# A mixture-of-experts stage with its loops written out, and one tile fewer

## The chip, the cores and the metric

The kernel runs on one core of a Trainium2 chip. The metric is the device time of one execution in microseconds (us). A core has five engines with programs of their own: TensorE (PE, matrix products; PEld is its weight load), VectorE (DVE), ScalarE (ACT), GpSimd (POOL) and SyncE (SP), which here does nothing but issue transfers. They wait for each other on semaphores.

## What is computed

One transformer layer on x of 4 x 1024 tokens of width 128, all in float32:

```python
x = _layernorm(x + attn(x, W_Q, W_K, W_V, W_O))     # 16 heads, rope, causal
gate_probs = softmax(x @ Wg + bg)                   # 8 experts
_, top_idx = top_k(gate_probs, 2)
selected = gate_probs * one_hot(top_idx).sum(-2)
selected = selected / (selected.sum(-1, keepdims=True) + 1e-08)
h = gelu(einsum('bsf,efh->bseh', x, W1) + b1)       # hidden width 512
expert_out = einsum('bseh,ehf->bsef', h, W2) + b2
x = _layernorm(x + einsum('bsef,bse->bsf', expert_out, selected))
```

## The kernel before

**Before the expert stage.** Attention runs as a long list of events, with batches 1 and 2 as two turns of a hardware loop. During it the router finds two experts for each token, and POOL scatters a row for each of the 8192 (token, expert) pairs into the DRAM buffer `pairs`, sorted by expert. This fills most of the time up to 568 us of the profiled execution.

**Tiles.** The expert stage works on tiles of 128 pairs that belong to one expert. 8192 pairs make 64 full tiles, and each of 8 experts can leave one more that is not full, so at most 64 + 8 - 1 = 71 tiles hold pairs. `NTILE` is this number rounded up to a whole turn of `TL` = 8 tiles: 72. Tiles count from 0; turn t is tiles 8t to 8t+7. Which expert a tile belongs to and where its rows stand is worked out on DVE (`word`, `expert`). The first `EARLY` = 40 tiles are filled from batches 0 to 2, and run while the routing of batch 3 is still going on; tiles from 40 on need all pairs.

**A tile's way.** SP (`load_pairs`, L606 to L614) reads the tile's word from memory into a register, waits until buffer k = tile mod 8 is free (`ys_ready` of the tile 8 before), then issues two transfers: the expert's weights W1 with biases into `w1e` (L612, 322 KB) and the 128 rows into `xg` (L613, 66 KB; the trace calls xg `region`). PE then does three things with each tile, and in one step of its program they belong to three tiles: `stage_down` of tile i (L832: reads the expert's number; L837: four products), `stage_up` of tile i+2 (L848: four products) and `stage_tx` of tile i+3 (L857: a transpose of the rows; it waits for the load). ACT copies the transpose (L923) and does four gelus, one for each quarter (L931). DVE (`stage_y`, L1357 to L1363) adds b2 and multiplies by the gate; POOL (`stage_out`, L1528) scatters the rows to `results`.

**The turns.** `pipeline` writes this out for each engine. A turn in which other work stands at fixed tiles (`TILE_EVENTS`: routing of batch 3 in turns 0 to 3, the sums of batches 0 to 2 at tiles 64 to 71), turn 4 and the last turn are written out tile by tile, so every number in them is a constant. Turns 5, 6 and 7 (tiles 40 to 63) are a hardware loop `Fori` of 8 tiles; there each semaphore count is `turn * 8 + k`, with the turn in a register. On SP the loads of tiles 8 to 31 and of tiles 40 to 63 are two such loops. Between them stand turn 4's loads, each followed by a transfer that pads one expert's rows (L633, L634), and a wait for all scatters (L636 to L638).

**The end.** After its load of tile 65, SP waits for the results of tiles up to 55 (L646) and reads the results of batch 0 back (`load_back`, L618, two transfers of 512 KB), after tiles 67 and 69 those of batches 1 and 2. POOL adds the first half of each (`FIRST`, L1511), DVE the second (`SECOND`, L1341), and DVE takes the statistics (`SUM`, L1346). `SCALES` makes the layernorm factors of batches 0 to 2, with which ACT normalises them (L943). When all results are out (L651), batch 3 is read back and treated in the same way (DVE L1372 to L1383).

Of the kernel before, what the change touches and what calls it, by code (L numbers as in the profile page):

```python
# [26 lines left out]
P = 128  # L27
B, S, D = 4, 1024, 128
H, DK = 16, 8
E, HID = 8, 512  # L30
# [15 lines left out]
GATE_EPS = 1e-8  # L46
TL = 8

NTILE = -(-(2 * B * S // P + E - 1) // TL) * TL
CAPT = B * S // P + 1  # L50
SPARE = NTILE - 2 * B * S // P

EARLY = (2 * (B - 1) * BT - (E - 1)) // TL * TL
LATE = NTILE - EARLY

OLD = -(-(2 * (B - 1) * BT + E - 1) // TL) * TL
# [159 lines left out]
def tile_events():  # L216

    groups = []
    for e, r in EVENTS[END + 1:]:
        if e[0] == "TILE":  # L220
            groups.append([])
        else:
            groups[-1].append((e, r))
    chain = [g for g in groups if g[0][0][0] != "SC"]
    plan = {}
    for i, g in enumerate(chain):
        plan.setdefault(2 * i // 3, []).extend(g)
    first = 2 * (len(chain) - 1) // 3 + 1
    scatters = [e for g in groups if g[0][0][0] == "SC" for e in g]
    for i, e in enumerate(scatters):  # L230
        plan.setdefault(first + i // 2, []).append(e)
    for i in range(4):
        plan.setdefault(first + i, []).append((("TB", i), None))
    done = max(plan)
    assert done < EARLY - TL + 2

    tail = {8: [("FIRST", 0)], 9: [("SECOND", 0), ("FIRST", 1)], 10: [("SUM", 0, 0), ("SUM", 0, 1)],
            11: [("SECOND", 1), ("FIRST", 2)], 12: [("SUM", 1, 0), ("SUM", 1, 1)], 13: [("SECOND", 2)],
            14: [("SUM", 2, 0), ("SUM", 2, 1)], 15: [("SCALES",), ("FIRST", B - 1)]}
# [40 lines left out]
def build(nc, xT, x, w, wg, bg, w1, w2,  # L280
          cs, ident, halves, maskA, before, tile128, tokens, tiles, first_row, out):
    ctx = ExitStack()
    with ctx:
# [199 lines left out]
        def _(sp):  # L483
# [121 lines left out]
            def load_pairs(turn, k):  # L605
                both = sp.value_load(word[0:1, bass.ds(turn * TL + k, 1)], min_val=0, max_val=E * PLACES - 1)  # L606
                t = (both & (PLACES - 1)).with_bounds(min_val=0, max_val=E * CAPT + SPARE - 1)
                e = (both >> 9).with_bounds(min_val=0, max_val=E - 1)
                if not (isinstance(turn, int) and turn == 0):
# [11 lines left out]

            sp.wait_ge(tiles_ready, 1)
            sp.wait_ge(pv_done, NB * (NU - 1))
            for k in range(TL):
                load_pairs(0, k)
            with sp.Fori(1, EARLY // TL - 1) as turn:
                for k in range(TL):
                    load_pairs(turn, k)

            sp.wait_ge(pad_ready, 1)  # L630
            for e_ in range(E):
# [4 lines left out]
            sp.wait_ge(tiles_ready, 2)  # L636
            sp.wait_ge(spare_in, 16 * (1 + E))
            sp.wait_ge(pairs_out, 16 * 2 * NT)  # L638
            with sp.Fori(EARLY // TL, NTILE // TL - 1) as turn:
                for k in range(TL):  # L640
                    load_pairs(turn, k)
            for k in range(TL):
# [21 lines left out]
        def _(pe):  # L664
# [187 lines left out]
            def stage_tx(turn, k):  # L852

                pe.wait_ge(pair_in[k], turn * 32 + 32)
                if not (isinstance(turn, int) and turn == k == 0):
# [154 lines left out]
        def _(ve):  # L1010
# [344 lines left out]
            def stage_y(turn, k):  # L1355
                ve.wait_ge(y_done, turn * TL + (k + 1))
                v.tensor_tensor(yb[:, k % 2, :], down[k % 2],  # L1357
                                w1e[:, k, HID + HC:HID + HC + D], ALU.add).then_inc(y_read, 1)
                if not (isinstance(turn, int) and turn == 0):
# [174 lines left out]

def first_use(turn, k):

    return isinstance(turn, int) and turn == 0 and k < 2


def first_late(turn, k):  # L1540

    return isinstance(turn, int) and turn * TL + k == EARLY


def pipeline(eng, stages, visit):

    lead = max(n for _, n in stages)
    turns = NTILE // TL

    for t in range(-lead, 0):  # L1550
        for stage, n in stages:
            if 0 <= t + n:
                stage(0, t + n)
    def whole(turn):
        for k in range(TL):
# [8 lines left out]
    single = {i // TL for i in TILE_EVENTS} | {EARLY // TL - 1, turns - 1}  # L1564
    turn = 0
    while turn < turns:
        if turn in single:
            whole(turn)
            turn += 1
        else:  # L1570
# [53 lines left out]
```

## Time and profile before

| | us |
|---|---|
| median of 3 runs | 769.34 |
| lowest, highest | 766.18, 774.05 |
| profiled execution, span | 795.5 |
| PE busy in the profiled execution | 670.2 (84%) |
| DVE busy | 570.4 (72%) |
| ACT busy | 443.8 (56%) |
| POOL busy | 351.2 (44%) |

All times in the text that are not called a run are those of the profiled execution, from the start of its span. The columns of each view are told where its first rows stand.

### The profile page before, as it was taken

Reading aid. Unit: us, or ns where it says so; the run is one execution under the profiler, and the core shown is the slowest. Engines: PE = TensorE matmul, PEld = TensorE weight load, DVE = VectorE, ACT = ScalarE, POOL = GpSimd, SP = SyncE. Lnnn points to the kernel's source line nnn. Section 1 sums busy time; section 2 is a strip of 40 time slices with the busy share of each in tenths; the row PEclk is TensorE's granted clock in tenths of the full one; section 3 lists DMA queues with packets and bytes.
Section 4 is the critical chain, followed back from the end, with each engine's and each line's share of the span. In section 5 each row is a group of like instructions: output and inputs, shape, how many; then the busy total and the mean of one; then the engine's idle time right before and its main releaser. Section 6 shows DMA issues by size and latency. Waiting matters only on the chain.

```text
span 795.5 us, 19063 instructions
## 1 busy us (share of the span) xinstructions
PE 670.2 (84%) x5560; PEld 362.2 (46%) x5561; DVE 570.4 (72%) x1386; ACT 443.8 (56%) x843; POOL 351.2 (44%) x664
## 2 busy tenths in 40 slices
PE   7879999999898897989898998898698766999950
PEld 3344333334343332434333334332198756888840
DVE  8977888888879886787988898986255621222295
ACT  2343676666555665555567656567456433655535
POOL 5862224223353484153447516248423555444460
PEclk9985999999989999898999999999799977999995
DMA  8883455011010120101012001000276745687935
GB/s 288 271 287 130 141 136 157 18 49 49 2 49 2 56 79 22 49 1 49 6 55 83 28 33 48 1 8 29 66 217 185 198 123 151 186 212 204 298 89 158
DMA packets 67358, 83.75 MB, mean 105 GB/s; under 512 B 9266, under 2 KB 46776, under 8 KB 67264
## 3 DMA queue, kind: packets, MB, share of 16 engines
q1 hardware_dynamic: 62912, 74.04, 31.5%
q0 software_dynamic: 4352, 8.53, 3.1%
q8 instruction: 49, 0.80, 0.5%
q14 instruction: 45, 0.37, 0.2%
HBM read 55.77 MB, written 26.90 MB: 104 GB/s over the span
## 4 chain that ended last, share of the span: by engine, by line
PE 53%; DVE 21%; issue 10%; ACT 4%; SPq 3%; DMA 3%; POOL 2%; another core or an unknown queue 1%; DVEq 0%; ACTq 0%; POOLq 0%
PE banks L779 15%; DVE mx L1226 12%; PE banks L729 9%; PE banks L759 6%; PE banks L837 5%; PE banks L848 5%; PE banks L724 3%; ACT region L895 2%; PE banks L671 2%; PE banks L788 2%; DMA region<-pairs 1%; DVE region L1363 1%; PE banks L686 1%; ACT region L931 1%
## 5 line engine op out<-in xcount | busy, mean ns | idle before, releaser
L1226 DVE TENSOR_REDUCE mx<-banks 128x1 f32<-128x512 f32 (+3 forms) x640 | 365.2, 631 | 52.3 <-PE banks L729 47.6
L895 ACT ACTIVATE region<-banks 128x1024 f32<-128x1024 f32 (+3 forms) x256 | 201.5, 841 | 136.8 <-PE banks L759 132.1
L729 PE MATMUL banks<-region 64*128 64x512 bf16 (+3 forms) x768 | 188.4, 340 | 13.8 <-DVE mx L1226 10.8
L759 PE MATMUL banks<-region 64*128 64x512 bf16 (+3 forms) x768 | 139.2, 339 | 12.0 <-ACT region L895 5.5
L779 PE MATMUL banks<-region 128*32 128x512 f32 (+3 forms) x1024 | 118.8, 537 | 0.9 <-POOL region L1518 0.8
L1528 POOL DMA_INDIRECT results<-region,dest x72 | 71.5, 993 | 105.8 <-DVE region L1363 83.8
L895 ACT ACTIVATE cs_sb<-banks 128x1024 f32<-128x1024 f32 (+2 forms) x128 | 91.2, 759 | 43.2 <-PE banks L759 42.4
L724 PE MATMUL banks<-mask_sb,half_sb 64*128 64x128 bf16 (+1 forms) x384 | 83.3, 249 | 25.4 <-DVE mx L1226 19.8
L1518 POOL TENSOR_SCALAR_AFFINE_SELECT region<-region 128x256 f32<-128x256 f32 x160 | 63.8, 407 | 84.0 <-ACT region L895 80.6
L848 PE MATMUL banks<-region,w1e 128*128 128x128 f32 x576 | 84.0, 293 | 20.0 <-ACT region L923 15.2
L1357 DVE TENSOR_TENSOR region<-banks,w1e 128x128 f32<-128x128 f32 x72 | 20.9, 290 | 105.6 <-PE banks L837 60.0
L1518 POOL TENSOR_SCALAR_AFFINE_SELECT cs_sb<-cs_sb 128x256 f32<-128x256 f32 x96 | 38.0, 408 | 128.6 <-ACT cs_sb L895 127.8
L759 PEld LDWEIGHTS banks<-region 64*128 64x128 bf16 x768 | 42.1, 94 | 112.8 <-issue 41.9
L837 PE MATMUL banks<-w_sb,region 128*128 x576 | 83.7, 291 | 7.9 <-DVE region L1357 3.1
L848 PEld LDWEIGHTS banks<-region,w1e 128*128 128x128 f32 x576 | 76.4, 207 | 22.3 <-ACT region L923 17.0
L729 PEld LDWEIGHTS banks<-region 64*128 64x128 bf16 x768 | 63.3, 98 | 49.4 <-DVE mx L1226 34.7
L931 ACT ACTIVATE region<-banks,w1e 128x128 f32<-128x128 f32 x288 | 82.6, 378 | 0.5 <-PE banks L848 0.5
L837 PEld LDWEIGHTS banks<-w_sb,region 128*128 128x128 f32 x576 | 74.4, 201 | 12.9 <-issue 11.5
L1503 POOL DMA_INDIRECT pairs<-xT_sb,slot x64 | 63.0, 985 | 24.4 <-issue 15.0
L923 ACT COPY region<-banks 128x128 f32<-128x128 f32 x72 | 19.2, 266 | 94.5 <-PE banks L857 62.2
L726 PE MATMUL banks<-mask_sb,half_sb 64*128 64x64 bf16 (+1 forms) x384 | 70.1, 207 | 0.0
L724 PEld LDWEIGHTS banks<-mask_sb,half_sb 64*128 64x128 bf16 x384 | 34.8, 97 | 62.4 <-DVE mx L1226 44.8
(204 smaller groups left out, 705.9 us busy)
## 6 DMA issues: line engine op xcount, KB each, us to landing
w1e<-in_w SPq DMA_DIRECT2D x72, 322.0 KB
region<-stack_q SPq DMA_DIRECT2D x64, 112.0 KB
region<-stack_k SPq DMA_DIRECT2D x32, 224.0 KB
region<-pairs SPq DMA_DIRECT2D x72, 66.0 KB
region<-results SPq DMA_DIRECT2D x8, 512.0 KB, 4.8
stack_q<-x_sb SPq DMA_DIRECT2D x8, 384.0 KB, 3.7
stack_k<-x_sb SPq DMA_DIRECT2D x8, 384.0 KB, 4.6
stack_q<-x_sb SPq DMA_DIRECT2D x8, 256.0 KB, 3.6
```

Source lines behind the costliest of these rows:

```text
L724: mm(view[:, :, n - P:n], half_sb[rows, 0, :], mask_sb[rows, 0, 0:k, :], start=True, stop=False, skip_group_check=True)
L726: mm(view[:, :, n - P // 2:n], half_sb[rows, 1, :], mask_sb[rows, 1, 0:k, P // 2:P], start=False, stop=False, skip_group_check=True)
L729: last = mm(ring[:, bank, m * n:(m + 1) * n], qst[rows, v % NG, sb_ // 4, slot_, sb_ % 4 * P:(sb_ % 4 + 1) * P], kst[rows, v % NG, slot_, ...
L759: last = mm(score[:, slot_, par, 0:n], kst[rows, u % NG, slot_, j * P:(j + 1) * P], qst[rows, u % NG, c, slot_, s0 - c * CH:s0 - c * CH + ...
L779: last = mm(pv[32 * h:32 * h + 32, s0 - c * CH:s0 - c * CH + n], vx[:, u % NG, j, h, :], probs[(2 * e[1] + slot_) % 6][:, par, 0:n], start ...
L837: last = mm(down[k % 2], hg[:, k % 2, hc * P:(hc + 1) * P], w2_sb[:, bass.ds(e, 1), hc, :].rearrange("p a n -> p (a n)"), start=(hc == 0), ...
L848: last = mm(hidden[k % 2][:, hc * P:(hc + 1) * P], w1e[:, k, hc * P:(hc + 1) * P], xgT[:, k % 2, :], start=(hc == 0), stop=(hc == HC - 1), ...
L895: nc.scalar.activation(probs[i % 6][:, :, 0:n], score[:, i % 2, :, 0:n], ACT.Exp, scale=SCALE).then_inc(exp_done, 1)
L931: nc.scalar.activation(hg[:, k % 2, cols], hidden[k % 2][:, cols], ACT.Gelu_apprx_tanh, bias=w1e[:, k, HID + hc:HID + hc + 1]).then_inc(ge ...
L1226: read(v.tensor_reduce(dst, src, AX.X, ALU.max, negate=True))
L1518: pp.affine_select(out=block_, in_=block_, compare_op=ALU.is_ge, fill=0.0, base=0, pattern=[[0, 2], [1, P]], channel_multiplier=-1).then_i ...
L1528: pp.indirect_dma_start(out=results, out_offset=bass.IndirectOffsetOnAxis(ap=dest[:, k, :], axis=0), in_=ys[:, k, :], in_offset=None, boun ...
```

## The change

`NTILE` becomes 71. All engines' turns are written out: `pipeline` has no loop any more, and so have SP's loads. `SCALES` and `FIRST` of batch 3 move from tile 71 to tile 70, behind that tile's `SUM`.

```diff
-NTILE = -(-(2 * B * S // P + E - 1) // TL) * TL
+NTILE = 2 * B * S // P + E - 1
...
-            14: [("SUM", 2, 0), ("SUM", 2, 1)], 15: [("SCALES",), ("FIRST", B - 1)]}
+            14: [("SUM", 2, 0), ("SUM", 2, 1), ("SCALES",), ("FIRST", B - 1)]}
...
-            with sp.Fori(EARLY // TL, NTILE // TL - 1) as turn:
-                for k in range(TL):
-                    load_pairs(turn, k)
-            for k in range(TL):
-                load_pairs(NTILE // TL - 1, k)
-                if k == 1:
+            for t in range(EARLY, NTILE):
+                load_pairs(t // TL, t % TL)
+                if t == NTILE // TL * TL + 1:
                     for i in range(TL):
                         sp.wait_ge(result_out[i], 16 * (OLD // TL))
-                if k in (1, 3, 5):
-                    load_back(k // 2)
+                if t - NTILE // TL * TL in (1, 3, 5):
+                    load_back(t % TL // 2)
 
             for k in range(TL):
-                sp.wait_ge(result_out[k], 16 * (NTILE // TL))
+                sp.wait_ge(result_out[k], 16 * (NTILE // TL + (k < NTILE % TL)))
...
-    for t in range(-lead, 0):
+    for t in range(-lead, NTILE):
         for stage, n in stages:
-            if 0 <= t + n:
-                stage(0, t + n)
-    def whole(turn):
-        for k in range(TL):
-            for stage, n in stages:
-                if not isinstance(turn, int) or turn * TL + k + n < NTILE:
-                    stage(turn + (k + n) // TL, (k + n) % TL)
-            if isinstance(turn, int):
-                for e, r in TILE_EVENTS.get(turn * TL + k, []):
-                    visit(e, r, lambda n, stride: n)
...
-            end = min(i for i in single if i > turn)
-            with eng.Fori(turn, end) as i:
-                whole(i)
-            turn = end
+            if 0 <= t + n < NTILE:
+                stage((t + n) // TL, (t + n) % TL)
+        for e, r in TILE_EVENTS.get(t, []):
+            visit(e, r, lambda n, stride: n)
```

On PE, the first tile of the loop's body before, from the loop's entry: the read of the expert's number, `stage_down`, and the beginning of `stage_up`. `REGISTER_ALU` and `ISA` are register instructions.

```order
2904 L1572 ISA
2905 L832 TENSOR_LOAD expert
2906 L832 ISA x2
2907 L834 REGISTER_ALU
2908 L836 ISA [waits y_read]
2909 L837 ISA [waits gelu_done]
2910 L837 MATMUL banks<-w_sb,region 128x128
2911 L836 REGISTER_ALU
2912 L837 ISA [waits gelu_done]
2913 L837 MATMUL banks<-w_sb,region 128x128
2914 L836 REGISTER_ALU
2915 L837 ISA [waits gelu_done]
```

The same piece of PE's program in the change, for a tile of the turns that were in the loop (its lines are 5 lower):

```order
2707 L827 TENSOR_LOAD expert
2708 L827 ISA x2
2709 L832 ISA [waits gelu_done,y_read]
2710 L832 MATMUL banks<-w_sb,region 128x128
2711 L832 ISA [waits gelu_done]
2712 L832 MATMUL banks<-w_sb,region 128x128
2713 L832 ISA [waits gelu_done]
2714 L832 MATMUL banks<-w_sb,region 128x128
2715 L832 ISA [waits gelu_done]
```

Gone are one register instruction ahead of each quarter's product, and others ahead of the first; the products, their number and their order are the same.

On SP, the last load of the loop's body before, the loop's end, and the first load of the last turn, which was written out already:

```order
504 L606 ISA
505 L606 TENSOR_LOAD word
506 L606 ISA x2
507 L612 ISA [waits ys_ready]
508 L612 DMA w1e<-in_w 128x644
509 L613 REGISTER_ALU
510 L613 ISA
511 L613 DMA region<-pairs 128x132
512 L639 REGISTER_ALU
513 L639 COMPARE_AND_BRANCH
514 L606 TENSOR_LOAD word
```

In the change every load has the form that the last turn's loads had:

```order
732 L607 TENSOR_LOAD word
733 L607 ISA x2
734 L613 ISA [waits ys_ready]
735 L613 DMA w1e<-in_w 128x644
736 L614 REGISTER_ALU
737 L614 ISA
738 L614 DMA region<-pairs 128x132
```

A load in the loop had a register instruction ahead of the read, most had another ahead of the wait, and every eighth had the branch.

## Rows read from the trace of the kernel before

**Rows 1.** The page: its span, its engines (busy us, share, instructions), one of its queues.

```profile
span 795.5 us, 19063 instructions
...
PE 670.2 (84%) x5560; PEld 362.2 (46%) x5561; DVE 570.4 (72%) x1386; ACT 443.8 (56%) x843; POOL 351.2 (44%) x664
...
q8 instruction: 49, 0.80, 0.5%
```

**Rows 2.** Chain of waits, 625 to 660 us: start, length, what the end waited for.

```profile
630.86 10.73 another core or an unknown queue
```

**Rows 3.** Timeline of PE: start, us, line, operation [idle before]; L857 is one per tile.

```profile
676.32 0.27 PE L857 MATMUL banks<-id_sb,region 128*128 128x128 f32 x1
...
687.69 0.27 PE L857 MATMUL banks<-id_sb,region 128*128 128x128 f32 x1
...
690.21 0.33 PE L857 MATMUL banks<-id_sb,region 128*128 128x128 f32 x1 [0.46 <-DMA region<-pairs]
...
693.02 0.27 PE L857 MATMUL banks<-id_sb,region 128*128 128x128 f32 x1
...
700.54 0.27 PE L857 MATMUL banks<-id_sb,region 128*128 128x128 f32 x1
...
712.84 0.27 PE L857 MATMUL banks<-id_sb,region 128*128 128x128 f32 x1
...
718.29 0.27 PE L857 MATMUL banks<-id_sb,region 128*128 128x128 f32 x1
...
741.99 0.27 PE L857 MATMUL banks<-id_sb,region 128*128 128x128 f32 x1
...
749.10 0.33 PE L857 MATMUL banks<-id_sb,region 128*128 128x128 f32 x1 [0.89 <-DMA region<-pairs]
...
752.81 0.42 PE L857 MATMUL banks<-id_sb,region 128*128 128x128 f32 x1
```

**Rows 4.** Stretch: busy us (instructions) of PE, PEld, DVE, ACT, POOL; clock, DMA share, GB/s.

```profile
674.30:687.69 13.39, 13.39 (x122) 13.39 (x121) 4.34 (x22) 9.15 (x35) 6.87 (x7) 1.00 0.59 168
```

**Rows 5.** Timeline of SP: weight loads of tiles 2, 3, then 42, 43, then 65.

```profile
575.65 0.33 SPq L612 DMA_DIRECT2D w1e<-in_w  x1
...
577.37 0.33 SPq L612 DMA_DIRECT2D w1e<-in_w  x1
...
690.84 0.33 SPq L612 DMA_DIRECT2D w1e<-in_w  x1
...
692.72 0.33 SPq L612 DMA_DIRECT2D w1e<-in_w  x1
...
740.04 0.17 SPq L612 DMA_DIRECT2D w1e<-in_w  x1
```

**Rows 6.** Waits of SP, 560 to 790: for what, us in total, times, longest.

```profile
SPq L612 <- DVE region L1363: 9.1, 6, 3.6
```

**Rows 7.** Timeline of DVE at the end.

```profile
754.91 0.29 DVE L1357 TENSOR_TENSOR region<-banks,w1e 128x128 f32<-128x128 f32 x1 [2.91 <-PE banks L837]
...
770.52 0.29 DVE L1357 TENSOR_TENSOR region<-banks,w1e 128x128 f32<-128x128 f32 x1
...
782.07 2.36 DVE L1372 TENSOR_TENSOR x_sb<-x_sb,region 128x512 f32<-128x512 f32 x2 [4.92 <-DMA region<-results]
```

**Rows 8.** Timeline of POOL at the end.

```profile
772.18 0.97 POOL L1528 DMA_INDIRECT results<-region,dest  x1 [0.84 <-DVE region L1363]
774.01 0.97 POOL L1528 DMA_INDIRECT results<-region,dest  x1 [0.86 <-DVE region L1363]
```

**Rows 9.** Timeline of PE at the first end of the attention loop's turn.

```profile
312.93 0.39 PE L759 MATMUL banks<-region 64*128 64x512 bf16 x2 [2.81 <-issue]
```

**Rows 10.** DMA queues, 309 to 314: packets, MB, share of 16 engines.

```profile
q8 instruction: 2, 0.03, 2.9%
```

**Rows 11.** DMA queues, 713 to 746, all that moved anything.

```profile
q1 hardware_dynamic: 5779, 6.46, 72.0%
q0 software_dynamic: 451, 0.81, 6.6%
```

More of the change, by code:

```diff
@@ L238, in tile_events @@
             11: [("SECOND", 1), ("FIRST", 2)], 12: [("SUM", 1, 0), ("SUM", 1, 1)], 13: [("SECOND", 2)],
-            14: [("SUM", 2, 0), ("SUM", 2, 1)], 15: [("SCALES",), ("FIRST", B - 1)]}
+            14: [("SUM", 2, 0), ("SUM", 2, 1), ("SCALES",), ("FIRST", B - 1)]}
+    assert max(tail) == NTILE - 1 - OLD
     for i, events in tail.items():
@@ L608, in load_pairs @@
                 e = (both >> 9).with_bounds(min_val=0, max_val=E - 1)
-                if not (isinstance(turn, int) and turn == 0):
+                if turn > 0:
                     sp.wait_ge(ys_ready, turn * TL + (k + 1 - TL))
@@ L623, in _ @@
             sp.wait_ge(pv_done, NB * (NU - 1))
-            for k in range(TL):
-                load_pairs(0, k)
-            with sp.Fori(1, EARLY // TL - 1) as turn:
-                for k in range(TL):
-                    load_pairs(turn, k)
+            for t in range(EARLY - TL):
+                load_pairs(t // TL, t % TL)
             sp.wait_ge(pad_ready, 1)
@@ L638, in _ @@
             sp.wait_ge(pairs_out, 16 * 2 * NT)
-            with sp.Fori(EARLY // TL, NTILE // TL - 1) as turn:
-                for k in range(TL):
-                    load_pairs(turn, k)
-            for k in range(TL):
-                load_pairs(NTILE // TL - 1, k)
-                if k == 1:
+            for t in range(EARLY, NTILE):
+                load_pairs(t // TL, t % TL)
+                if t == NTILE // TL * TL + 1:
                     for i in range(TL):
                         sp.wait_ge(result_out[i], 16 * (OLD // TL))
-                if k in (1, 3, 5):
-                    load_back(k // 2)
+                if t - NTILE // TL * TL in (1, 3, 5):
+                    load_back(t % TL // 2)
             for k in range(TL):
-                sp.wait_ge(result_out[k], 16 * (NTILE // TL))
+                sp.wait_ge(result_out[k], 16 * (NTILE // TL + (k < NTILE % TL)))
             load_back(B - 1)
@@ L854, in stage_tx @@
                 pe.wait_ge(pair_in[k], turn * 32 + 32)
-                if not (isinstance(turn, int) and turn == k == 0):
+                if turn or k:
                     pe.wait_ge(xgT_ready, turn * TL + k)
@@ L1358, in stage_y @@
                                 w1e[:, k, HID + HC:HID + HC + D], ALU.add).then_inc(y_read, 1)
-                if not (isinstance(turn, int) and turn == 0):
+                if turn > 0:
                     ve.wait_ge(result_out[k], turn * 16)
@@ L1535, in first_use @@
 def first_use(turn, k):
-    return isinstance(turn, int) and turn == 0 and k < 2
+    return turn == 0 and k < 2
 def first_late(turn, k):
-    return isinstance(turn, int) and turn * TL + k == EARLY
+    return turn * TL + k == EARLY
 def pipeline(eng, stages, visit):
     lead = max(n for _, n in stages)
-    turns = NTILE // TL
-    for t in range(-lead, 0):
+    for t in range(-lead, NTILE):
         for stage, n in stages:
-            if 0 <= t + n:
-                stage(0, t + n)
-    def whole(turn):
-        for k in range(TL):
-            for stage, n in stages:
-                if not isinstance(turn, int) or turn * TL + k + n < NTILE:
-                    stage(turn + (k + n) // TL, (k + n) % TL)
-            if isinstance(turn, int):
-                for e, r in TILE_EVENTS.get(turn * TL + k, []):
-                    visit(e, r, lambda n, stride: n)
[L1564 to L1570, printed above, removed]
-            end = min(i for i in single if i > turn)
-            with eng.Fori(turn, end) as i:
-                whole(i)
-            turn = end
+            if 0 <= t + n < NTILE:
+                stage((t + n) // TL, (t + n) % TL)
+        for e, r in TILE_EVENTS.get(t, []):
+            visit(e, r, lambda n, stride: n)
 def kernel(L0_attn_x, L0_attn_W_Q, L0_attn_W_K, L0_attn_W_V, L0_attn_W_O, L0_ffn_Wg, L0_ffn_bg,
```

## The prediction, made before the change was run

> **What bounds the kernel now.** I read the page first. PE is the busiest engine, with 84% of a span of 795.5 us [rows 1], and most of that is attention, which the change does not touch. Then I read the chain of waits over the expert stage. Its largest piece is 10.73 us at 630.86 in which nothing that the profile shows was waited for [rows 2]. The median of the runs is 769.34, 26 us under the profiled span, so 26 us of the profiled execution are not in the timed ones. I take stalls of this kind for most of them and claim nothing from them. This one lies in turns that were written out already.
>
> The question is then what one tile costs in each turn. PE's transpose L857 comes once a tile, so its starts in PE's timeline are a clock of the stage. In turn 4, written out before, it goes from 676.32 to 687.69 in 6 tiles: 1.895 us a tile [rows 3]. Over that stretch PE is busy 13.39 of 13.39 us at the full clock [rows 4]. So a written-out turn runs at PE's own work, and no other engine holds it.
>
> From tile 40 on this changes. Tile 40's transpose waits 0.46 us for its load, at 690.21 (SP had pads and a wait for all scatters ahead of it). From tile 41 at 693.02 to tile 63 at 741.99 it takes 48.97 us for 22 tiles, 2.23 a tile. A calm piece inside a turn, 700.54 to 712.84, is 6 tiles in 12.30 us: 2.05 a tile. The two tiles behind it, where the first turn ends, take 5.45 us (to 718.29) [rows 3].
>
> **The change, part by part.**
>
> *Register work of the loop on PE.* 2.05 against 1.895 is 0.155 us a tile. The order listing has a register instruction ahead of the `stage_down` products and more at the other waits, and nothing else differs for PE between turn 4 and these turns: same products, same waits. 22 tiles by 0.155 = 3.4 us. In the change this costs nothing, as in turn 4.
>
> *The turns' ends.* 48.97 - 22 x 2.05 = 3.9 us remain. 1.35 of it stand around the first turn's end (5.45 - 2 x 2.05). From 693.02 to 700.54 3 tiles take 7.52 us, 1.37 over the loop's pace: that is PE getting its lead back after tile 40, with loads that arrive one by one. The rest, 1.15, is spread over the second and third turn. I claim the first turn's end (1.35), half of the rest (0.6), and a quarter of the restart (0.35), as SP's faster loads help there: 2.3 us. Together 5.7 us, of at most 48.97 - 41.69 = 7.3.
>
> *Loads.* Where SP waits for nothing, one written-out load takes 1.72 us (575.65 to 577.37), and one in the loop 1.88 (690.84 to 692.72) [rows 5]. For tiles 8 to 31 the 0.16 us buy nothing: SP waits there for free buffers, 9.1 us in six waits [rows 6], and what it gains it waits longer. Without that cover it would be 24 x 0.16 = 3.8 us. From tile 40 on SP has little lead. At 1.88 it is faster than PE's 2.05, at 1.72 faster than 1.895, by about the same, so PE's pace is not SP's. It matters at one place. Tile 65's load is issued at 740.04, tile 66's comes behind the two read-back transfers, and PE stands 0.89 us for it at 749.10. From 741.99 to 749.10 3 tiles take 7.11 us, 1.4 more than at 1.895, and the next takes 3.71 (752.81), 1.8 more [rows 3]. Bounds: 0, if in timed runs SP is in time anyway, and 3.2, if all this lateness goes. SP took 49.2 us from tile 42 to tile 65, 2.14 a tile where undisturbed loads take 1.88; if that is disturbance that only the profiled run has, SP is in time in the others. The term is then nearer its lower end, and I take 1.0.
>
> *One tile fewer.* In the last turn DVE goes from tile 65's `stage_y` at 754.91 to tile 70's at 770.52, 3.1 us a tile [rows 7]; its `SECOND` and `SUM`, and waits beside POOL's `FIRST`, lie between. So DVE sets the end there, not PE. Tile 71 comes last with no sum beside it: POOL's scatters of tiles 70 and 71 start at 772.18 and 774.01 [rows 8], and the wait for all results hangs on the last. This removes 1.83 us. Bounds: 0.6, DVE's and POOL's part alone if they ran side by side (two operations of 0.29), and 3.1, a mean tile of that stretch; the pair of scatters is the nearest row.
>
> *`SCALES` one tile earlier.* DVE stands 4.92 us before the read-back of batch 3 arrives at 782.07 [rows 7]. Both `SCALES`, ahead of this wait, and the read-back move by the same tile. Cost nothing; if `SCALES` came 4.92 us later it would begin to show. `FIRST` of batch 3 on POOL waits for that read-back anyway.
>
> *More code.* The three turns are three times as long in memory. The trace shows what a fetch costs when it is in the way: at the first turn end of the attention loop PE stands 2.81 us with "issue" as the reason [rows 9], and two packets of the instruction queue q8 fall into this stretch [rows 10]. In the expert loop, from 713 to 746, only q1 and q0 move anything [rows 11]: no code was fetched at its turns. Turn 4 is straight code at PE's full pace, so I cost the straight code at nothing, with a bound of 2.81 for each block that comes late.
>
> The Trainium skill (Runtime: NRT & Kernel Launch, "Instruction fetch mechanics") says that engines prefetch code in sequence, and that a taken branch to code outside the window at hand forces a fetch first. For the attention loop the trace agrees (2.81 us). Held against the expert loop, two taken branches would cost 5.6 us instead of the 1.95 that I claim at turn ends, and the time would be 757.1; the rows of the queues speak against it here.
>
> **Sum:** 3.4 + 2.3 + 1.0 + 1.8 = 8.5 us. Against the profile's own span, 795.5 - 8.5 = 787.0. The terms are tiles at an undisturbed pace, so I carry them over whole to the runs: 769.34 - 8.5 = 760.8 us, 1.1% faster. All of it must get through to the end. It does if the last turn moves as a whole: the read-backs are issued behind tile 65's load, which comes earlier with both PE and SP, and DVE's stretch starts when tile 64 and the first read-back are there.
>
> **Rivals.**
>
> *The loop's cost was hidden, and only the tile counts.* For it: SP delivered at 2.14 us a tile, near PE's 2.23, and q1 fills 72% of the DMA engines' time [rows 11], so PE may have followed the loads. Against it: PE's timeline has one wait for a load in these turns, the 0.46 at tile 40. Then 1.8 us and perhaps a third of the rest (6.7 / 3 = 2.2) are gained: 765.3, within 1%.
>
> *The slower one: code comes late.* Place: turns 5 to 8, on PE or SP, when transfers of loads and read-backs stand before the code's. Price: 2.81 us a block. PE's two extra turns are 16 tiles of 17 products and 17 weight loads, 544 instructions; q8 moved 49 packets for PE's 11,121 [rows 1], so two or three more, and SP's may be as many. With three late nothing is left of the gain; with six, 769.34 - 8.5 + 16.9 = 777.7, slower by 1.1%. Against it: turn 4 and most of attention are straight code that came in time.
>
> *More is gained.* Tile 66's load is late in the timed runs as well, and all loss at turns goes: 7.3 + 3.2 + 1.8 = 12.3, 757.0.
>
> **How the numbers follow.** Main case, 758.5 to 764: 0.55. Hidden cost, 764 to 768: 0.22. More, under 758.5: 0.15. Late code: 0.08, mostly above 768. The predicted time is 760.8. The range for 8 in 10 goes from 756.5, the larger gain with 0.5 for the spread of the runs, to 767.5, the tile alone; it leaves out most of the late code and the edges of its neighbours, 0.18. A measurement of this kernel can tell about 1% from no change, and 1% is at 761.65. Of the main case 0.34 lies below it, with the larger gain 0.49: faster. Slower, above 777: 0.04. The same: 0.47.
>
> **What would show it.** L857 should go at 1.90 us from tile 41 to 63, in under 43.5 us, with no gap at tiles 48 and 56, and SP's loads at 1.72 where nothing is waited for: that proves the first 5.7 us. A pace of 2.05 with PE waiting for `xg` would prove the first rival; gaps with "issue" beside instruction packets, the second. Tile 66's transpose without a wait, where before it had one, proves the 1.0. The last scatter should be tile 70's, and DVE's read-back sum 8 us after it, as before (774.01 to 782.07). The prediction is wrong if the last turn starts earlier but ends at the old time, because loads and read-backs, not DVE, set the pace there.

## The result, and the profile after

The changed kernel takes 764.91 us in the median of 18 runs (759.32 to 770.69); the kernel before takes 771.14 in 18 (764.83 to 777.0). The ratio is 0.9917, 95% interval 0.9893 to 0.9941: 0.8% faster, which is 6.4 us of 771.14, with 6.2 between the two medians. The prediction was 760.8 with a range of 756.5 to 767.5. Ratios and means of runs leave out executions that took over 1.5% more than the fastest of their kernel in the same comparison; medians are of all.

The page after: span, engines, and one queue.

```profile
span 766.1 us, 18659 instructions
...
PE 660.7 (86%) x5543; PEld 357.4 (47%) x5543; DVE 570.3 (74%) x1383; ACT 441.7 (58%) x838; POOL 350.6 (46%) x663
...
q8 instruction: 51, 0.84, 0.5%
```

404 instructions are gone, and q8 moved 2 packets more than the 49 of before [rows 1]. This queue brings PE's code: it moves 49 packets in e4 below, where PE alone keeps its loop, and 51 in e7, where PE alone is written out. The span is 29 us under that of the first profile. That is far more than the runs differ by, so spans can't be subtracted here. A profiled execution's own time, where it is known, is its span and 1.8 us; what the first profile had too much is settled below with two more profiles of the kernel before.

PE's timeline after, the transposes (they were L857, now L852) of tiles 40 to 43, 63 and 65 to 68:

```profile
668.64 0.47 PE L852 MATMUL banks<-id_sb,region 128*128 128x128 f32 x1 [3.51 <-DMA region<-pairs]
...
673.10 0.42 PE L852 MATMUL banks<-id_sb,region 128*128 128x128 f32 x1
...
675.96 0.27 PE L852 MATMUL banks<-id_sb,region 128*128 128x128 f32 x1
...
677.86 0.27 PE L852 MATMUL banks<-id_sb,region 128*128 128x128 f32 x1
...
715.77 0.27 PE L852 MATMUL banks<-id_sb,region 128*128 128x128 f32 x1
...
719.56 0.27 PE L852 MATMUL banks<-id_sb,region 128*128 128x128 f32 x1
...
721.61 0.33 PE L852 MATMUL banks<-id_sb,region 128*128 128x128 f32 x1
722.48 1.15 PE L832 MATMUL banks<-w_sb,region 128*128 x8 [0.54 <-issue]
...
724.36 0.27 PE L852 MATMUL banks<-id_sb,region 128*128 128x128 f32 x1
...
727.81 0.33 PE L852 MATMUL banks<-id_sb,region 128*128 128x128 f32 x1 [1.39 <-DMA region<-pairs]
```

From 675.96 to 715.77 there are 21 tiles in 39.81 us: 1.896 each, the pace of turn 4 [rows 3], with no gap at tiles 48 and 56 or anywhere else. Over the same stretch, busy us (instructions) of PE, PEld, DVE, ACT, POOL, then clock, DMA share, GB/s:

```profile
674.00:714.00 40.00, 40.00 (x356) 40.00 (x356) 13.12 (x63) 27.04 (x104) 19.68 (x21) 0.99 0.87 243
```

PE is never idle. And yet code was fetched meanwhile; the queues of these 40 us (packets, MB, share of 16 engines), where the loop before fetched none from 713 to 746, with two turns' ends in it [rows 11]:

```profile
q1 hardware_dynamic: 6082, 8.39, 78.4%
q0 software_dynamic: 637, 1.22, 8.1%
q8 instruction: 4, 0.07, 0.7%
q14 instruction: 3, 0.02, 0.1%
```

At the end, DVE's `stage_y` of tile 70 and POOL's last scatter, which now is tile 70's:

```profile
742.80 0.29 DVE L1352 TENSOR_TENSOR region<-banks,w1e 128x128 f32<-128x128 f32 x1
...
752.63 2.36 DVE L1367 TENSOR_TENSOR x_sb<-x_sb,region 128x512 f32<-128x512 f32 x2 [3.67 <-DMA region<-results]
```

```profile
744.46 0.97 POOL L1523 DMA_INDIRECT results<-region,dest  x1 [0.85 <-DVE region L1358]
```

The last scatter stands 1.66 us behind this `stage_y`; before it was 3.49 (770.52 to 774.01) [rows 7, 8]. From it to the read-back's sum on DVE are 8.17 us, before 8.06. DVE waits 3.67 us for the read-back, before 4.92 [rows 7]: `SCALES` is still hidden.

### The profile page after: what moved, and what is told of

Its sections match the earlier page's. It is cut to its first block, busy times and chain, and to the rows that moved or that the text cites. A ratio compares the mean times of both kernels' runs of the same rounds, so it can differ in the third digit from the quotient of the medians.

```text
span 766.1 us, 18659 instructions
## 1 busy us (share of the span) xinstructions
PE 660.7 (86%) x5543; PEld 357.4 (47%) x5543; DVE 570.3 (74%) x1383; ACT 441.7 (58%) x838; POOL 350.6 (46%) x663
## 4 chain that ended last, share of the span: by engine, by line
PE 57%; DVE 21%; issue 8%; SPq 4%; DMA 3%; ACT 3%; POOL 2%; DVEq 0%; POOLq 0%; ACTq 0%
PE banks L774 15%; DVE mx L1221 13%; PE banks L724 9%; PE banks L832 6%; PE banks L843 6%; PE banks L754 6%; PE banks L666 3%; PE banks L719 3%; PE banks L783 2%; ACT region L890 2%; PE banks L681 2%; SPq L613 1%; DMA region<-pairs 1%; PE banks L812 1%; PE banks L790 1%
## 5 line engine op out<-in xcount | busy, mean ns | idle before, releaser
L774 PE MATMUL banks<-region 128*32 128x512 f32 (+3 forms) x1024 | 116.5, 528 | 0.9 <-POOL region L1513 0.8
L832 PE MATMUL banks<-w_sb,region 128*128 x568 | 79.6, 286 | 5.5 <-issue 3.3
L843 PE MATMUL banks<-region,w1e 128*128 128x128 f32 x568 | 78.9, 284 | 1.0 <-ACT region L918 1.0
L832 PEld LDWEIGHTS banks<-w_sb,region 128*128 128x128 f32 x568 | 72.2, 199 | 8.3 <-issue 8.2
L843 PEld LDWEIGHTS banks<-region,w1e 128*128 128x128 f32 x568 | 72.5, 200 | 1.9 <-ACT region L918 1.9
```

Source lines behind the costliest of these rows:

```text
L774: last = mm(pv[32 * h:32 * h + 32, s0 - c * CH:s0 - c * CH + n], vx[:, u % NG, j, h, :], probs[(2 * e[1] + slot_) % 6][:, par, 0:n], start ...
L832: last = mm(down[k % 2], hg[:, k % 2, hc * P:(hc + 1) * P], w2_sb[:, bass.ds(e, 1), hc, :].rearrange("p a n -> p (a n)"), start=(hc == 0), ...
L843: last = mm(hidden[k % 2][:, hc * P:(hc + 1) * P], w1e[:, k, hc * P:(hc + 1) * P], xgT[:, k % 2, :], start=(hc == 0), stop=(hc == HC - 1), ...
```

## The experiments

Segments of every profile, in us, worked out from the starts of the transposes (tx) of the named tiles, of `stage_y` (y) and of the last scatter. A transpose begins in this table with its weight load (PEld), 0.1 us ahead of the product that the lines show and 0.2 ahead at half the clock; so 42.77 stands here where the lines give 42.67 (673.10 to 715.77). "24-41" is tx of tile 24 to tx of tile 41, and so on; "load 0" is the time at which SP issues the first load.

| kernel | ratio to before, 95% | load 0 | tx 24-41 | tx 41-63 | tx 63-y 65 | y 65-y 70 | y 70-last scatter | scatter-end | tx 41-end |
|---|---|---|---|---|---|---|---|---|---|
| before, first profile | | 572.1 | disturbed | 48.97 | 13.03 | 15.61 | 3.48 | 21.51 | 102.60 |
| e1, before again | 0.9988 (0.9951-1.0025) | 560.4 | 42.65 | 46.70 | 9.45 | 17.25 | 3.48 | 21.44 | 98.31 |
| e6, before again | one run, 773.82 | 569.6 | 45.11 | 46.22 | 9.47 | 17.23 | 3.48 | 21.47 | 97.87 |
| the change | 0.9917 (0.9893-0.9941) | 569.3 | 44.21 | 42.77 | 9.90 | 17.24 | 1.66 | 21.61 | 93.18 |
| e5, the change again | 0.9839 (0.9777-0.9900) | 565.2 | 42.65 | 42.57 | 10.03 | 17.23 | 1.66 | 21.83 | 93.32 |
| e2, 71 tiles alone | 0.9946 (0.9906-0.9987) | 565.8 | 42.86 | 45.70 | 9.64 | 17.23 | 1.66 | 21.55 | 95.77 |
| e3, written out alone | 0.9940 (0.9903-0.9977) | 565.0 | 44.46 | 42.77 | 8.90 | 17.24 | 3.47 | 21.44 | 93.82 |
| e4, only PE in a loop | 0.9959 (0.9922-0.9997) | 564.6 | 42.26 | 45.94 | 9.43 | 17.23 | 1.66 | 21.52 | 95.77 |
| e7, only PE written out | 0.9931 (0.9898-0.9963) | 568.4 | 44.91 | 42.95 | 11.41 | 17.24 | 1.66 | 21.77 | 95.03 |
| e8, pads early | 0.9823 (0.9773-0.9873) | 568.7 | 37.87 | 43.30 | 10.16 | 17.24 | 1.66 | 21.63 | 93.98 |
| e9, pads spread | 0.9816 (0.9758-0.9874) | 569.4 | 37.89 | 42.77 | 13.52 | 15.79 | 1.65 | 21.46 | 95.21 |
| e10, `FIRST` on DVE | 0.9881 (0.9811-0.9951) | 564.1 | 42.79 | 41.92 | 8.90 | 13.64 | 1.67 | 21.63 | 87.75 |
| e11, e9 and e10 | 0.9809 (0.9757-0.9861) | 568.7 | 38.35 | 41.71 | 9.57 | 14.33 | 1.67 | 21.71 | 88.99 |
| e12, pads on ACT too | 0.9773 (0.9724-0.9822) | 563.6 | 34.90 | 42.59 | 11.34 | 14.88 | 1.67 | 21.89 | 92.37 |

Where nothing was edited, the segments from tile 41 on repeat to 0.5 us (tx 41-63 of the kernel before: 46.70 and 46.22, of the change: 42.77 and 42.57; y 65-y 70: 17.23 to 17.25). The runs of the change have 11 us between the fastest and the slowest. So the segments tell apart what single runs can't.

The means of all runs say more, since the granted clock of every run is on record with it. The mean time and clock: before 770.9 at 0.940 (81 runs of the comparisons below), the change 763.8 at 0.940 (23, with those of e5), so 7.2 us less at the same clock. For the others an estimate, from a line fitted to these runs (4.0 us for 0.01 of clock), says how much less than before they take at equal clock: e2 2.5, e3 5.1, e4 3.3 and e7 3.0 us, each within 1 us.

**e1, e6: the kernel before, again.** No edit.

> The kernel before, unchanged, for a second profile, since the first one had a span of 795.5 us against runs of 765 to 777. My theory (the 26 us are stalls of that one execution, mostly at tiles 21 to 31): a span of 763 to 777; turns 5 to 7 (tiles 41 to 63) still at 2.0 to 2.1 us a tile, 45 to 47 us for 22 tiles where the first profile had 48.97; ratio to before 1.00. Rival (the pace of 2.05 was itself part of the disturbance): 1.90 to 1.95 a tile, 42 to 43 us.

> The kernel before, a third profile. Theory A: tile 32 to 41 in 26.8 to 28.9 us, with half clock or without. Theory B: 27.1 as in the second profile, no half clock there. Both: 46 to 47.5 us for tiles 41 to 63, 98 from tile 41 to the end.

Measured: 770.27 (ratio 0.9988), spans 760.6 and 772.0. In both, tiles 41 to 63 take 46.2 to 46.7 us, not 48.97, and tile 66 doesn't wait. From e1's PE timeline: tiles 41 to 43; tiles 50 and 51 with what lies between; tile 52; tiles 53, 57 and 58; tile 59; tile 63; tiles 65 and 66.

```profile
662.37 0.27 PE L857 MATMUL banks<-id_sb,region 128*128 128x128 f32 x1
...
664.42 0.27 PE L857 MATMUL banks<-id_sb,region 128*128 128x128 f32 x1
...
667.24 0.27 PE L857 MATMUL banks<-id_sb,region 128*128 128x128 f32 x1
...
681.79 0.27 PE L857 MATMUL banks<-id_sb,region 128*128 128x128 f32 x1
682.43 1.16 PE L837 MATMUL banks<-w_sb,region 128*128 x8 [0.38 <-issue]
683.42 1.06 PE L848 MATMUL banks<-region,w1e 128*128 128x128 f32 x8
684.32 0.27 PE L857 MATMUL banks<-id_sb,region 128*128 128x128 f32 x1
...
686.50 0.27 PE L857 MATMUL banks<-id_sb,region 128*128 128x128 f32 x1
...
688.49 0.27 PE L857 MATMUL banks<-id_sb,region 128*128 128x128 f32 x1
...
696.59 0.27 PE L857 MATMUL banks<-id_sb,region 128*128 128x128 f32 x1
698.59 0.27 PE L857 MATMUL banks<-id_sb,region 128*128 128x128 f32 x1
...
701.01 0.27 PE L857 MATMUL banks<-id_sb,region 128*128 128x128 f32 x1
...
709.07 0.27 PE L857 MATMUL banks<-id_sb,region 128*128 128x128 f32 x1
...
713.16 0.27 PE L857 MATMUL banks<-id_sb,region 128*128 128x128 f32 x1
...
715.15 0.27 PE L857 MATMUL banks<-id_sb,region 128*128 128x128 f32 x1
```

Inside a turn 4 tiles take 8.10 us (688.49 to 696.59): 2.025 each. A turn's end makes one tile of it 2.53 (681.79 to 684.32) or 2.42 (698.59 to 701.01), 0.45 more on average. The 0.38 us idle there are "issue": PE waited for no other engine that the profile shows. The 2.05 a tile and the 1.35 for the first turn's end of the prediction were read from a disturbed execution: the end itself took 2.55 there as well (712.84 to 715.39), and the tile behind it 2.90 (to 718.29), where e1 has 2.18 (684.32 to 686.50).

**e2, e3: each half of the change alone.** e2 takes 71 tiles into the kernel before; e3 writes all turns out and keeps 72.

```diff
e2, against before
-NTILE = -(-(2 * B * S // P + E - 1) // TL) * TL
+NTILE = 2 * B * S // P + E - 1
...
-            14: [("SUM", 2, 0), ("SUM", 2, 1)], 15: [("SCALES",), ("FIRST", B - 1)]}
+            14: [("SUM", 2, 0), ("SUM", 2, 1), ("SCALES",), ("FIRST", B - 1)]}
...
-    turns = NTILE // TL
+    turns = -(-NTILE // TL)
```

> The kernel before with 71 tiles and its loops kept (SCALES at tile 70). My theory: the last tile is worth the 1.8 us between the last two scatters, so 769.3 us where before has 771.1, ratio 0.9976. Rival (the last tile is hidden beside the read-backs): 1.000. Rival (a mean tile of DVE's last stretch, 3.1): 0.996.

> The change without its smaller number of tiles: all turns written out, 72 tiles. My theory: the difference of the whole change, 6.4, less 1.8, so 4.6 us faster than before, ratio 0.994, tiles 41 to 63 at 1.90 us. Rival (the loop's cost was hidden, only the tile counts): 1.000 here.

Measured: 766.29 (0.9946) and 767.97 (0.9940). Their intervals overlap nearly whole, but the segments part them: from tile 41 to the end e2 takes 2.3 us less than the mean of e1 and e6 (98.09), 1.82 of them at the last scatter, and e3 takes 4.3 less, 3.7 of them in tiles 41 to 63. In e3 the last scatter is 3.47 behind `stage_y` of tile 70, as before. The two halves act in different places and don't need each other. In the runs at equal clock they add up, 2.5 + 5.1 against 7.2. In the profiles they don't, 2.3 + 4.3 against 4.8 for the whole: e3 takes 8.90 us from tx 63 to y 65 and the change 9.90 and 10.03, though the loads up to there are the same. That piece is taken up at tile 66 below.

**e4: the change, but PE keeps its loop over tiles 40 to 63.** (The same pipeline function takes a list of the engines that loop.)

```diff
+LOOPED = ('stage_tx3',)
...
+        if t == EARLY and stages[-1][0].__qualname__.split(".")[-1] + str(len(stages)) in LOOPED:
+            with eng.Fori(EARLY // TL, EARLY // TL + 3) as turn:
+                for k in range(TL):
+                    step(None, turn, k)
```

> The changed kernel, but PE alone keeps a hardware loop for tiles 40 to 63; the other engines and SP are written out. My theory (PE's register work in the loop costs 0.15 a tile and its turn ends about 1 each): most of the gain of writing out is lost, ratio to before 0.997, tiles 41 to 63 at 2.05 to 2.15. Rival (the loads, that is SP's loop, set the pace): 0.992, as the change, at 1.90.

Measured: 766.29 (0.9959), and 45.94 us for tiles 41 to 63, as in e2 (45.70), though ACT, DVE, POOL and SP were written out. So none of these four held the turns, and with PE in its loop, writing them out gains nothing: 95.77 us from tile 41 to the end in both.

**e7: the counterpart, PE alone written out.** ACT, DVE, POOL and SP loop as before.

```diff
+LOOPED = ('stage_gelu2', 'stage_y1', 'stage_out1')
...
-            for t in range(EARLY, NTILE):
+            with sp.Fori(EARLY // TL, NTILE // TL) as turn:
+                for k in range(TL):
+                    load_pairs(turn, k)
...
```

> The changed kernel (71 tiles), but PE alone is written out; ACT, DVE, POOL and SP keep their loops, SP both of its own. My theory (only PE's own register work counts): 42.8 to 43.5 us for tiles 41 to 63, as the change; ratio to before 0.992 to 0.994. Rival (a chain over ACT and DVE, or SP's 1.88 a load, holds PE as soon as it is faster): 44 to 46 us.

Measured: 767.74 (0.9931). Tiles 41 to 63 take 42.95 us, within 0.4 of the change: up to tile 63 the gain of the turns is PE's own. Most of it is given back behind that, where PE now stands for tile 66's load:

```profile
723.16 0.33 PE L858 MATMUL banks<-id_sb,region 128*128 128x128 f32 x1 [0.98 <-DMA region<-pairs]
```

tx 63 to y 65 is 11.41 here and 9.90 to 10.03 in the change. SP issues the load of tile 65 only 1.6 us ahead of tile 63's transpose, in the change 3.4 to 3.7 and in e2 5.0: a faster PE uses up SP's lead, and SP's loop, at 1.86 us a load against 1.72, can't make it up. So PE alone brings 0.7 us from tile 41 to the end (95.03 against 95.77 in e2), and the other engines' part, made on top of it, 1.8 (93.25), of which 1.4 lie at this place. The runs say it more strongly: at equal clock e4 and e7 are within 1 us of e2, and the change is 4.2 us faster than e7 (estimate as above, within 1.1). The gain of writing out needs PE and the engine that feeds it together. What of the 4.2 doesn't lie in the 1.8 is not located.

**e5: the change again.** No edit. The change's profile has 4.46 us from tile 40 to 41 (668.64 to 673.10), at the lower clock level; the question was whether the change brings this.

> The changed kernel again, for a second profile. In its first profile tile 41 comes 28.7 us after tile 32, 1.6 more than in the second profile of before, and PE's clock is at half for 6.8 us from tile 40 on; the same in the kernel with 72 tiles and everything written out. Theory A (the half clock after the idle stretch before tile 40 comes by chance and not from the change): this profile may lie anywhere between 26.8 and 28.9, with the half clock between 0 and 6.8 us. Theory B (the written-out code loses 1.6 us here each time): 28.5 to 28.9 again. Both: 42.8 us for tiles 41 to 63, 93.2 from tile 41 to the end but for the clock; ratio 0.992.

Measured: 762.36 (0.9839), span 759.9. The stretch from 668 to 675 in the change, with the granted clock as the third number from the end:

```profile
668.00:675.00 7.00, 5.94 (x26) 5.65 (x27) 0.61 (x3) 2.62 (x10) 3.03 (x4) 0.52 0.89 246
```

The same 7 us of the change again (e5):

```profile
668.00:675.00 7.00, 6.68 (x60) 6.45 (x59) 2.39 (x12) 4.24 (x17) 3.34 (x4) 1.00 0.93 279
```

And of the kernel before again (e6):

```profile
668.00:675.00 7.00, 4.70 (x21) 4.41 (x22) 0.62 (x3) 1.50 (x7) 3.12 (x4) 0.56 0.85 240
```

In all three PE stood for tile 40's load just before, 3.51, 1.75 and 4.51 us. Behind that stop the clock fell to about half, which is the level of 1.2 GHz, in the change and in the kernel before, and didn't in the change again. The kernel before had both cases too: in e1 the stop was 2.20 us, and the next tile came 2.88 us later at the full clock. So this is not the change's; it is part of the spread of the runs. Attention gives most of the rest: from 0 to 565 us the mean clock is 0.97 in e1 and 0.95 in e6 and the change, and load 0 is issued at 560.4, 569.6 and 569.3. Where an execution starts its expert stage varies by 12 us; that is why the median of a few runs can miss a gain of 5.

**e8, e9: the pads earlier.** In the change PE stands longest ahead of tile 40 (3.51 us above). SP issues a pad behind each load of tiles 32 to 39, and then waits for all of them. SP's waits between 600 and 700 us, total, times, longest:

```profile
SPq L613 <- DVE region L1358: 7.3, 10, 1.9
SPq L636 <- DMA pairs<-pad: 3.6, 1, 3.6
```

e8 puts the pads behind the loads of tiles 26 to 33, e9 behind 26, 27, 29, 30, 32, 33, 35 and 36.

```diff
+PADS = 26
...
-            for t in range(EARLY - TL):
+            for t in range(EARLY):
                 load_pairs(t // TL, t % TL)
...
-            for e_ in range(E):
-                load_pairs(EARLY // TL - 1, e_)
...
+                e_ = t - PADS
...
+                if 0 <= e_ < E:
...
```

> The changed kernel, with the eight pads behind the loads of tiles 26 to 33 instead of 32 to 39. PE stands before tile 40 because SP issues load and pad at 2.9 us a tile there, and then waits 3.6 us for the pads to land. My theory: tile 40's load comes 14 to 17 us after tile 32's transpose instead of 21.5, set by the last scatters, and the whole is 5 us faster than the change: ratio to before 0.985, ratio to the change 0.993. Rival (the scatters on POOL hold tile 40 as long as the pads do): 20 to 21.5, no gain. Rival (SP now starves PE before tile 34): tile 24 to 32 longer than the 15.5 us of all others, and half of the gain lost.

> The changed kernel with the eight pads behind the loads of tiles 26, 27, 29, 30, 32, 33, 35 and 36. With the pads at 26 to 33 PE still lost 1.9 us between tiles 24 and 32 and 3.4 between 32 and 41, since SP needed 2.9 us a tile for eight tiles running. My theory (SP's issue time is what PE waits for, spread out it fits into SP's lead): tiles 24 to 41 in 33 to 35 us, where the change takes 43 to 44 and the pads at 26 to 33 took 37.9 (PE's own pace would be 32.2); ratio to before 0.975 to 0.98. Rival (the last scatters of pairs hold tile 40's load): 36 to 38, as with the pads at 26 to 33.

Measured: 760.98 (0.9823) and 758.67 (0.9816). The wait for the pads is gone in both, and tiles 24 to 41 take 37.9 us in both, against 42.65 to 45.11. e8 came out as expected (0.985 or better), though tiles 24 to 32 take 17.29 us there against 15.47, as its second rival said. e9 missed its 33 to 35 us and came out at the number of its rival, but not for the rival's reason: SP waits for no scatter there. That the two agree so closely speaks against the idea that spacing the pads matters; what is left is SP's issue time in sum, which e12 tests. With a pad a load takes 2.9 us (SP issues e8's first pads at 624.65, 627.51 and 630.37), against PE's 1.895 a tile. A part of the gain is given back in e9, where tx 63 to y 65 is 13.52. (The profiled execution of e9 was the slowest of its six, so its end is the least sure of the table.)

**e10: `FIRST` of batches 0 to 2 on DVE.** y 65 to y 70 is 17.24 us in every undisturbed profile of before and of the change, whatever the loads do. The reason stands on DVE, `stage_y` of tile 65 and what follows:

```profile
725.57 0.29 DVE L1352 TENSOR_TENSOR region<-banks,w1e 128x128 f32<-128x128 f32 x1 [1.28 <-PE banks L832]
725.77 0.14 DVE L1356 COPY dest<-region 128x1 int32<-128x1 int32 x1
725.89 2.63 DVE L1358 TENSOR_SCALAR region<-region 128x128 f32<-128x128 f32 x1
728.47 1.23 DVE L1336 TENSOR_TENSOR x_sb<-x_sb,region 128x1024 f32<-128x1024 f32 x1
```

and on POOL beside it:

```profile
726.06 2.37 POOL L1506 TENSOR_TENSOR x_sb<-x_sb,region 128x1024 f32<-128x1024 f32 x1
```

The multiplication L1358 takes 0.29 us elsewhere; beside POOL's `FIRST` it takes 2.63, 2.79 and 2.64, and ends when POOL's does. (The Trainium skill, SBUF — State Buffer, section "Who interferes with whom": VectorE in a two-port mode, which `tensor_scalar` can enter, and GpSimd share a pair of ports that one of them holds for a whole instruction, while the other is fully blocked. The trace agrees in that 0.29 us became 2.63, up to the end of POOL's instruction, and not a share of both. Who took the ports first it doesn't show: DVE's record begins 0.17 us ahead of POOL's.)

```diff
+                elif kind == "FIRST" and e[1] < B - 1:
+                    b = e[1]
+                    ve.wait_ge(back_in[b], 32)
+                    mine = x_sb[:, b * BT:(b + 1) * BT, :]
+                    v.tensor_tensor(mine, mine, back[b][:, 0, :, :], ALU.add).then_inc(first_added, 1)
...
-                elif e[0] == "FIRST":
+                elif e[0] == "FIRST" and e[1] == B - 1:
```

> The changed kernel, with the first halves of the sums of batches 0 to 2 (FIRST) on DVE instead of POOL; in the last turn DVE's multiply L1358 takes 2.6 to 2.8 us instead of 0.29 whenever POOL adds, so three sums cost DVE 7.3 us in all where 3 x 1.22 of its own would do. My theory (DVE sets the end): tile 65's to tile 70's stage_y in 13 to 14 us instead of 17.24, 3 to 4 us faster, ratio to before 0.987. Rival (loads and read-backs on full DMA engines set it): 16 to 17 us, under 1 us faster.

Measured: 764.16 (0.9881). `FIRST` takes 1.22 us on DVE, and the multiplication (here L1363) is at most 0.55 from tile 65 to 70:

```profile
715.55 1.22 DVE L1336 TENSOR_TENSOR x_sb<-x_sb,region 128x1024 f32<-128x1024 f32 x1
716.92 0.29 DVE L1357 TENSOR_TENSOR region<-banks,w1e 128x128 f32<-128x128 f32 x1 [0.15 <-PE banks L832]
717.13 0.14 DVE L1361 COPY dest<-region 128x1 int32<-128x1 int32 x1
717.24 0.43 DVE L1363 TENSOR_SCALAR region<-region 128x128 f32<-128x128 f32 x1
```

y 65 to y 70 is 13.64, so 3.6 us of the profile are gained, and tile 41 to the end takes 87.75. The six runs reach from 755.6, which is the profiled one, to 794.4, and the median's ratio lies between those of the change and of the change again (e5), so the ratio confirms no amount. The four runs behind that ratio have a mean of 760.7 at a clock of 0.940, 3.1 us under the change's at the same clock, which fits the 3.6; but four are few. The trace shows the mechanism, and its worth in time is about this size.

**e11, e12: together.** e11 is e9 with e10. e12 takes the pads off SP: ACT issues one in each of its steps 24 to 31.

```diff
e12, against e11
-PADS = (26, 27, 29, 30, 32, 33, 35, 36)
+PADS = (24, 25, 26, 27, 28, 29, 30, 31)
...
+    for e_, t in enumerate(PADS):
+        plan.setdefault(t, []).append((("PAD", e_), None))
...
+                elif e[0] == "PAD":
+                    e_ = e[1]
+                    if e_ == 0:
+                        act.wait_ge(pad_ready, 1)
+                    row = act.value_load(pad_row[0:1, e_:e_ + 1], min_val=0, max_val=(E * CAPT - 1) * P)
+                    act.dma_start(pairs[bass.ds(row, P), :], pad[:, :]).then_inc(spare_in, 16)
```

> The changed kernel with both: the pads spread as in the run before last, and FIRST of batches 0 to 2 on DVE. My theory: the two gains lie in stretches one behind the other and add up; about 12 us faster than the change, ratio to before 0.970 to 0.977. Rival (an earlier last turn meets later read-backs, so that part of the first gain is lost at the end): 0.978 to 0.982.

> As e11 (FIRST of batches 0 to 2 on DVE), but ScalarE reads the pads' rows and issues the eight pads, in its steps of tiles 24 to 31, and SP issues loads only. With the pads at other places of SP's list tiles 24 to 41 took 37.9 to 38.4 us twice, and SP waited for nothing before tile 40's load. Theory (what is short is SP's issue time in sum, 1.15 us a pad): 33.5 to 35.5 us here, ratio to before 0.976. Rival (the last scatters come just then and hold tile 40's load): 37 to 38. Rival (the eight pads hold ScalarE, which has 0.5 us a tile to spare, and with it PE): tiles 24 to 32 in 18 us or more instead of 15.8.

Measured: 756.91 (0.9809) and 752.59 (0.9773, 0.9724 to 0.9822), the best of all kernels here. e11 missed its 0.970 to 0.977 and lies where its rival put it: the two gains don't add up whole. With SP free, tiles 24 to 41 take 34.90 us against 38.35; ACT's pads cost 0.7 us in tiles 24 to 32 (16.48; e9 has 15.82). The row of the stretch in which the pads are issued, with the DMA share last but one, says what held PE and what no longer does; first the change, then e12:

```profile
639.00:661.00 22.00, 18.56 (x155) 17.32 (x154) 5.95 (x27) 12.51 (x49) 16.81 (x18) 1.00 0.76 210
```

```profile
628.00:645.00 17.00, 16.51 (x145) 16.02 (x145) 5.30 (x25) 10.84 (x42) 13.04 (x14) 1.00 0.96 279
```

With SP as the issuer of all, the DMA engines were 76% busy and PE stood 3.44 of 22 us; with ACT's help they are at 96%, and PE stands 0.49 of 17. So here PE's own work sets the pace again, with the DMA engines close to full. Now POOL's scatters hold SP ahead of tile 40, and not the pads; SP's waits from 600 to 700 in e12:

```profile
SPq L616 <- DVE region L1366: 6.0, 9, 1.5
SPq L633 <- DMA pairs<-xT_sb,slot: 5.2, 1, 5.2
```

At the end part of it is given back: tx 63 to y 65 is 11.34, and from load 0 to the end e11 and e12 take the same (186.6 and 186.5 us; the change 196.7 and 194.7, before 200.2 and 202.4). e12 is 4 us below e11 in the runs, but the intervals overlap, so this last step is not shown.

## Why the prediction was right, point by point

The time lies in the range, and the mechanism is the one forecast for PE and for the last tile; the sum was too high. From tile 41 to the end, mean of the change's two profiles (93.25) against that of e1 and e6 (98.09): 4.84 us. Up to tile 41 nothing differs beyond the spread (tx 24 to 41: 42.65 and 45.11 before, 44.21 and 42.65 after). 4.84 is at the lower end of what the first runs allow, for 0.9941 and 0.9893 of 771.14 are 4.5 and 8.3 us, and under what e5's interval allows (0.9900: 7.7 us). The 7.2 us of all runs at equal clock are the better figure for the whole, so about 2 us of the gain are in no row of this table. A part of them is which executions were profiled: by the line through the runs, e1's is 1.4 us faster than its kernel's usual one at that clock, and those of the change are 0.7 and 0.9 slower. Either way the 8.5 were too much.

| term | predicted | measured | from |
|---|---|---|---|
| register work of PE's loop | 3.4 | 2.9 | 22 x (2.025 - 1.895) |
| turns' ends, restart | 2.3 | 0.9 | 2 x 0.45 (e1) |
| tile 66's load late | 1.0 | -0.5 | tx 63 to y 65: 9.46 to 9.97 |
| last tile | 1.83 | 1.82 | y 70 to last scatter |
| behind the last scatter | 0 | -0.3 | 21.46 to 21.72 |
| sum | 8.5 | 4.8 | |

- **Register work.** Right in kind, and e4 and e7 show from both sides that it is PE's: 45.94 us with PE alone in the loop, 42.95 with PE alone written out. The term was mis-sized by 0.025 us a tile. The split between this term and the next hangs on one calm stretch of e1; measured is their sum, 3.8 us from tile 41 to 63 (46.46 - 42.67), where 5.7 was forecast.
- **Turns' ends.** Mis-sized, and this is the step that failed most: "1.35 of it stand around the first turn's end". The undisturbed ends cost 0.51 and 0.40. The restart behind tile 40 is not the loop's: one tile of 2.8 us stands there with the loop (664.42 to 667.24 in e1, at the full clock) and one without it (673.10 to 675.96, at half the clock), and e2, with the loop, has none (1.92 and 1.95 us for the two tiles behind tile 41). The first profile's 48.97 held 2.5 us that its kernel doesn't have in the other two. The prediction set 26 us of that profile aside as stalls and then read its small terms from the same stretch; the doubt had to go to these as well.
- **Tile 66.** The term came out with the wrong sign in both profiles of the change. The kernel before has no wait there in e1 and e6, so the sign that the prediction named, a transpose without a wait, proves nothing. In the change PE runs up to the load again (2.05 and 2.14 us from tile 65 to 66, then 2.75 and 2.79 to tile 67, against 1.99 and 2.06 in e1). That a faster PE must do so is not shown: e3 and e10, with the same loads and the same PE up to there, have 8.90 us from tx 63 to y 65, which would be +0.6. (tx 63 to y 65 holds 0.3 us of PE's own gain as well, since PE's loop ran up to tile 66's transpose: tiles 63 to 65 take 3.79 us in the change and 4.09 in e1. So the loss in the change is 0.8.) The loss goes with SP's lead: the load of tile 65 is issued 5.4 us ahead of tile 63's transpose in these two and in e6, 3.4 to 3.7 in the change, and 1.6 in e7, the worst. What sets this lead from one execution to the next stays open. The prediction took SP's part as a term of its own, of 1.0; by e7 it is rather the condition for PE's. From tile 65 on DVE sets the pace: y 65 to y 70 is 17.24 in the undisturbed profiles of before and of the change, with loads early or late.
- **Last tile.** Right to 0.01 us, and e2 and e3 show it by itself.
- **`SCALES` and the code at nothing.** Right. 4 packets of PE's code came within 40 us in which PE was never idle.
- **Rivals.** "Hidden cost" falls with e3 and e4; only with PE alone written out (e7) do the loads hide most of the gain. "Late code" falls with the queues; "more is gained" falls with the table and with the 7.2 us of the runs.
- **The median.** 764.91 is further from 760.8 than from the 765.3 of the first rival, though that rival's mechanism is refuted: 771.14 less 4.84 to 7.2 is 766.3 to 763.9, and 764.91 lies between. Of the 4.1 us between forecast and median, 1.8 are the kernel before, whose median was 771.14 in 18 runs and 769.34 in the 3 that the prediction started from. A time near a rival's doesn't prove the rival.

## What to carry to other kernels

A hardware loop of small steps costs what its register instructions add on the engine that sets the pace, here 0.13 us a tile and 0.45 a turn. On the engines that feed it the loop costs nothing while they are ahead, but once the pace rises it can hold the gain back, so write out both; the order of instructions says where, and a written-out turn in the same trace says how much. Small terms must not be read from a profile whose span is far off the runs: one more profile of the kernel before would have shown 46.5 for 48.97. And the next gains stood in the trace outside the change: an issuing engine with a second job (2.9 us a load against 1.9 a tile), and an elementwise operation that takes nine times its time beside another engine's.

## What the runs showed of the hardware

- A 128x128 multiplication on DVE of 0.29 us took 2.63 to 3.00 (e1) beside a 128x1024 addition on POOL of 2.37, and the same addition took 1.22 on DVE: all of the work on one engine (3.6 us less for five tiles) beat its division over two.
- The granted clock behind PE's stop ahead of tile 40 was 0.52 in one execution of the changed kernel (stop of 3.51 us) and 1.00 in another (1.75), 0.56 in one of the kernel before (4.51): the same code in the same place, with 4.46 us for a tile or 2.77.
- SP needs 1.72 us to issue a tile's two loads where each takes a register for its address, 1.86 to 1.88 in a loop, and 2.9 with a third transfer. This set the pace ahead of tile 40, while the DMA engines were 76% busy. With the third transfer issued by ACT they stood at 96%, and PE was busy for 16.51 of 17 us.
